# Attention on one core: maxima 4 units ahead instead of 6, rows turned two steps ahead instead of three, sums over V in halves in plain steps

## The chip, the cores and the metric

The kernel runs on one core of a Trainium2 chip. The metric is the device time of one execution in microseconds (us), the median of three runs. A core has TensorE (PE in the rows, its weight loads PEld), VectorE (DVE), ScalarE (ACT), GpSimd (POOL) and SyncE (SP), each with its own queue of instructions, worked through in order and held together by semaphores, and 16 DMA engines that they share.

## What is computed

Two transformer layers on x of 2 x 1024 x 288, each modulated by a condition vector. Both begin with an attention of 16 heads of 18 columns; layer 0 goes on with a dense MLP, layer 1 with a mixture of 4 experts of which each token takes 2. The change is in the attention alone, which is the same in both layers:

```python
qkv = (h @ W_qkv + b_qkv).reshape(B, N, 3, 16, 18)       # B = 2, N = 1024
scores = einsum('bhqd,bhkd->bhqk', q, k) * 18 ** -0.5
attn = softmax(scores, axis=-1)
o = einsum('bhqk,bhkd->bhqd', attn, v).reshape(B, N, 288)
x = x + gate * (o @ W_proj + b_proj)
```

## The kernel before, in words

`attention_stage` is called once for each layer. Its work is cut into 16 **spans**: 8 groups of 4 heads (`GROUPS`), each for 2 halves of 512 queries (`HALVES`). A span has 8 **steps** (`KT`), one for each block of 128 keys, so a layer has 128 steps.

Queries and keys lie as fp32r parts, two heads to a tile, one head in rows 0 to 55 and one in rows 64 to 119 (`QS`, `KS`). A step computes, for the 4 heads of its group:

- the scores of 128 keys against 512 queries, one matmul a head (`score`, L1101), into one of 3 PSUM banks `psS`. The maximum of each query is subtracted by the matmul itself, through two more rows of `QS` that hold the negated maxima in two parts;
- the exponentials of each, by ScalarE, from PSUM into `PR` (L972);
- the sums over V (`weigh`, L1112) of the step before: four matmuls of 32 output columns, which fill the array side by side (`tile_position=(0, 32 * j)`), accumulated over the 8 steps of a span in the bank `psO`. V holds a column of ones, so the sums of exponentials come out as well.

The maxima need a pass of their own. A **unit** is 128 queries of one head against all 1024 keys: two matmuls of 512 keys (`max_half`, L1062) into one of the two double banks `psM`, and one reduction on VectorE (L987). A span needs 16 units, and each step does two of them for a later span. `AHEAD` says how many units beyond the first span's 16 are done before the first step. When the 16 units of a span are through, `turn` (L1072) transposes the 128 x 16 maxima into the ring `psM`, VectorE splits them into two parts (`rows_out`, L997 and L999), SyncE stores them with four DMAs into the rows of `QS` (`store_max`, L832), and the first `score` of the span waits for these DMAs (`m_loaded`). `TURN_LEAD` says at the end of which step `turn` stands, counted back from the span's first. `spread` (L1081) is the matmul that spreads the inverted sums of the span before, at the end of a span's step 7 (`SPREAD_LAG`), and `divide` (L1017) uses it. SyncE's other work in a span is the load of the sums (L841) and two stores of their inverses (L846), around steps 1 to 5.

The order on each engine is written out by hand. On TensorE a step reads score 0, first half of a unit, score 1, second half, score 2, first half of the next unit, score 3, second half, `weigh` of the step before, and then `turn` or `spread` where there is one. The heads are taken in the order 0, 2, 1, 3, and a unit is of the head in the other rows, so that a score and the half unit behind it use different rows of the array and run together. I call such a couple a pair; a step has pairs 0 to 3. The waits that matter here:

```python
pe.wait_ge(exp_done, HG * st + n - 2)     # score(st, n): bank free, i.e. exponential of three scores ago done
pe.wait_ge(ring_read, ring - 1)           # max_half(q, 0): reduction of two units ago done
pe.wait_ge(exp_done, HG * (st + 1))       # weigh(st): all four exponentials of its step
pe.wait_ge(m_loaded[half], 64 * g + 64)   # score(8 * span, 0): the span's maxima are in QS
```

`TAIL` is the first step that has no units left. Spans, steps and pairs are counted from 0.

Of the kernel before, what the change touches and what calls it, by code (L numbers as in the profile page):

```python
# [32 lines left out]
BLK = 512  # L33
# [5 lines left out]
HG = 4  # L39
GPB = H // HG  # L40
GROUPS = B * GPB
KT = SEQ // P
# [655 lines left out]
STEPS = SPANS * KT  # L698
UNITS = HG * TPB
PER_STEP = UNITS // KT  # L700
AHEAD = 6
TURN_LEAD, COPY_LAG, RECIP_LAG, SPREAD_LAG = 3, 1, 4, 7


def unit_at(q):
# [6 lines left out]
def units_of(st):  # L712

    first = UNITS + AHEAD + PER_STEP * st
    return range(first, min(first + PER_STEP, SPANS * UNITS))
# [10 lines left out]
def span_turned(st):  # L726

    span, rest = divmod(st + TURN_LEAD, KT)
    return span if rest == 0 and 0 < span < SPANS else None
# [33 lines left out]
def attention_stage(nc, T, l, W, pieces):  # L763
# [4 lines left out]
    with ExitStack() as ctx:  # L768
# [276 lines left out]
        def _(pe):  # L1045
# [56 lines left out]
                                 QS[g % SLOTS][rows, half, p, :], start=True, stop=True  # L1102
                                 ).then_inc(scores_ready, 1)

            def weigh(st):
                span, k = divmod(st, KT)
                g = span // HALVES
                if k == 0 and span:
                    pe.wait_ge(oz_ready, span)
                pe.wait_ge(exp_done, HG * (st + 1))  # L1110
                for j in range(HG):
                    last = nc.tensor.matmul(psO[32 * j:32 * j + 32, :], T.V[:, g, k, 32 * j:32 * j + 32],  # L1112
                                            PR[st % 2][:, j, :], start=(k == 0), stop=(k == KT - 1),
                                            tile_position=(0, 32 * j))
                last.then_inc(pv_done, 1)

            def unit(q):
                max_half(q, 0)
# [5 lines left out]
                    turn(0)  # L1124
            for st in range(STEPS):
                units = list(units_of(st))
                score(st, 0)
                if units:
                    max_half(units[0], 0)
                score(st, 1)  # L1130
                if units:
                    max_half(units[0], 1)
                score(st, 2)
                if units:
                    max_half(units[1], 0)
                score(st, 3)
                if units:
                    max_half(units[1], 1)
                if st:
                    weigh(st - 1)  # L1140
                if (span := span_turned(st)) is not None:
                    turn(span)
                if (span := span_behind(st, SPREAD_LAG)) is not None:
                    spread(span)
            weigh(STEPS - 1)
            pe.wait_ge(oz_ready, SPANS)
            ring_free()
            nc.tensor.matmul(psM[ring % 2][:, 0, :], T.sel[:], OZ[HALVES - 1][:], start=True, stop=True
# [998 lines left out]
```

## Time and profile before

| what | us |
|---|---|
| median of three runs (lowest, highest) | 1590.88 (1589.6, 1596.12) |
| the profiled execution's own time | 1594.51 |
| its span, first to last instruction | 1592.8 |
| attention of layer 0, first reduction to last exponential | 136.0 to 514.7 |
| attention of layer 1, the same | 791.1 to 1172.6 |

The profile is of one execution. Its page gives the busy time of each engine; the timeline gives each instruction's start and length, and in brackets how long its engine had been idle and what ended that. TensorE's clock is granted at 1.00 (2.4 GHz) or 0.50 (1.2 GHz). A TensorE record's end is modelled, so its start is the better mark, and a matmul whose weights were not loaded ahead starts together with its weight load. An fp32 matmul stands in the records as two, which is why `weigh` has x8 in the timeline and x2048 on the page.

### The profile page before, as it was taken

To read this page: it belongs to the slowest core of one execution; us is meant where nothing else is said; L and a number is where in the kernel's file an instruction comes from. 1 tells how busy PE (TensorE), PEld (TensorE's weight loads), DVE (VectorE), ACT (ScalarE), POOL (GpSimd) and SP (SyncE) were. 2 spreads that over 40 slices of the span, in tenths; PEclk is the share of its full clock that TensorE was granted. 3 is DMA by queue.
4 is the path that set the end of the run, shared out by engine and by line. 5 is a ranking of instruction groups with operands and counts; after the bars stand their busy time and mean duration, and the time that the engine had idled before them with its cause. 6 is when DMAs were issued, how large, how long until landed. Compare 5 with 4: busy or idle time off the path is not lost. (4 is left out here: it accounts for less than half of the span.)

```text
span 1592.8 us, 25033 instructions
## 1 busy us (share of the span) xinstructions
PE 1383.1 (87%) x8657; PEld 867.5 (54%) x8657; DVE 1132.8 (71%) x1859; ACT 798.8 (50%) x1537; POOL 643.0 (40%) x857
## 2 busy tenths in 40 slices
PE   4686899999999879968799999999987299999995
PEld 2463333333332668856533333333335299999995
DVE  3756799999993546776489999999827456666663
ACT  0440577777778242224337677777854233332331
POOL 0433654431000515542469889888005511212121
PEclk7796899999999979989869999999998599999997
DMA  7475544331100249516561122220039456767672
GB/s 191 135 197 123 121 86 131 96 77 26 24 3 3 79 140 320 170 48 206 168 109 30 32 36 47 48 48 3 3 125 337 161 177 214 216 208 223 201 219 77
DMA packets 92740, 193.31 MB, mean 121 GB/s; under 512 B 35670, under 2 KB 62360, under 8 KB 89628
## 3 DMA queue, kind: packets, MB, share of 16 engines
q1 hardware_dynamic: 61020, 118.75, 23.2%
q0 software_dynamic: 31600, 73.00, 19.9%
q8 instruction: 70, 1.15, 0.3%
q14 instruction: 50, 0.41, 0.1%
HBM read 126.10 MB, written 66.67 MB: 121 GB/s over the span
## 5 line engine op out<-in xcount | busy, mean ns | idle before, releaser
L987 DVE TENSOR_REDUCE att_neg_max<-att_for_max 128x1 f32<-128x1024 f32 x512 | 601.0, 1219 | 74.2 <-PE att_for_max L1062 71.6
L972 ACT ACTIVATE att_probs<-att_scores 128x512 f32<-128x512 f32 x1002 | 525.1, 607 | 216.1 <-PE att_scores L1101 215.3
L1112 PE MATMUL att_out<-att_probs,V 128*32 128x512 f32 x2048 | 276.2, 612 | 2.9 <-ACT att_OZ L965 1.9
L1062 PE MATMUL att_for_max<-att_KS,att_QS 54*128 54x512 f32 x640 | 241.6, 461 | 3.7 <-DVE att_neg_max L987 2.5
L1101 PE MATMUL att_scores<-att_QS,att_KS 56*128 56x512 f32 x618 | 227.7, 450 | 18.2 <-ACT att_probs L972 16.1
L1101 PEld LDWEIGHTS att_scores<-att_QS,att_KS 56*128 56x128 f32 x618 | 101.8, 184 | 174.7 <-ACT att_probs L972 158.3
L1948 ACT ACTIVATE experts_gelu<-experts_proj,experts_b 128x256 f32<-128x256 f32 x171 | 81.3, 476 | 207.6 <-PE experts_proj L2017 186.8
L1062 PE MATMUL att_for_max<-KS,QS 54*128 54x512 f32 x384 | 162.8, 526 | 21.1 <-PEq L119 11.1
L2017 PE MATMUL experts_proj<-experts_x_parts,w_parts 128*128 128x256 f32 (+1 forms) x1197 | 173.9, 286 | 1.4 <-DVE experts_x_parts L1742 1.4
L1896 POOL DMA_INDIRECT sums_of_experts<-experts_y,experts_rows x38 | 61.1, 1607 | 259.2 <-DVE experts_y L1778 253.4
L2017 PEld LDWEIGHTS experts_proj<-experts_x_parts,w_parts 128*128 128x128 f32 (+1 forms) x1197 | 157.8, 191 | 5.4 <-issue 5.4
L1101 PE MATMUL att_scores<-QS,KS 56*128 56x512 f32 x384 | 147.1, 456 | 13.9 <-ACT att_probs L972 10.8
L1750 DVE CAST perts_hidden_parts<-experts_gelu 128x256 fp32r<-128x256 f32 x171 | 51.7, 302 | 110.9 <-ACT experts_gelu L1948 91.4
L1101 PEld LDWEIGHTS att_scores<-QS,KS 56*128 56x128 f32 x384 | 67.3, 190 | 109.6 <-ACT att_probs L972 93.2
L1062 PEld LDWEIGHTS att_for_max<-att_KS,att_QS 54*128 54x128 f32 x640 | 105.7, 185 | 24.1 <-DVE att_neg_max L987 19.1
L897 POOL TENSOR_TENSOR att_router_products<-att_router_products 128x576 f32<-128x576 f32 (+1 forms) x224 | 110.8, 495 | 17.6
L456 POOL DMA_DIRECT2D att_QS<-qk_halves x120 | 74.3, 653 | 107.2 <-PE att_scores L1101 81.3
L1062 PEld LDWEIGHTS att_for_max<-KS,QS 54*128 54x128 f32 x384 | 70.9, 217 | 57.9 <-DVE att_neg_max L987 43.9
L681 PE MATMUL qkv_qk<-qkv_hT_parts,qkv_wqkv_parts 128*126 128x512 f32 (+2 forms) x280 | 70.4, 406 | 14.3 <-DVE qkv_hT_parts L415 9.2
L1112 PEld LDWEIGHTS att_out<-att_probs,V 128*32 128x32 f32 x2048 | 40.4, 108 | 71.3 <-ACT att_probs L972 48.8
L1752 DVE TENSOR_TENSOR perts_hidden_parts<-experts_gelu,perts_hidden_parts 128x256 fp32r<-128x256 f32 x171 | 72.8, 426 | 5.8
L456 POOL DMA_DIRECT2D QS<-qk_halves x72 | 44.4, 645 | 75.8 <-PE att_scores L1101 42.0
(244 smaller groups left out, 2048.6 us busy)
## 6 DMA issues: line engine op xcount, KB each, us to landing
w_parts<-w_parts SPq DMA_DIRECT2D x19, 2304.0 KB
qk_halves<-qkv_qk_parts SPq DMA_DIRECT2D x40, 288.0 KB
w_parts<-w_parts SPq DMA_DIRECT2D x4, 2592.0 KB
slot_rows<-mlp_blank_rows SPq DMA_DIRECT2D x2, 5145.0 KB, 38.6
att_QS<-qk_halves POOLq DMA_DIRECT2D x120, 72.0 KB, 4.5
att_KS<-qk_halves POOLq DMA_DIRECT2D x60, 144.0 KB, 4.9
w_parts<-w_parts SPq DMA_DIRECT2D x19, 432.0 KB
experts_rows<-slot_rows SPq DMA_DIRECT2D x19, 294.0 KB
```

The lines of the kernel that those rows point to most:

```text
L456: eng.dma_start(Q[rows, half, :, :].bitcast(F32), heads[0, q, i, :, :, half * BLK:(half + 1) * BLK]).then_inc(sem, 16)
L681: last = nc.tensor.matmul(psQ[c % QK_BANKS][0:r, :], w[0:rows, ws, c0:c0 + r], hT[0:rows, hs, at:at + BLK], start=(n == 0), stop=(n == len ...
L897: at = router(nc.gpsimd.tensor_tensor(prod[:, 0:half, :], prod[:, 0:half, :], prod[:, half:2 * half, :], ALU.add))
L972: nc.scalar.activation(PR[st % 2][:, j, :], score_bank(st, n), ACT.Exp, scale=SCALE).then_inc(exp_done, 1)
L987: nc.vector.tensor_reduce(negm[half][:, c:c + 1], psM[ring % 2][:].rearrange("p a n -> p (a n)"), AX_X, ALU.max, negate=True).then_inc(rin ...
L1062: last = nc.tensor.matmul(psM[ring % 2][:, keys, :], QS[s][rows, half, p, t * P:(t + 1) * P], KS[s][rows, p, keys * BLK:(keys + 1) * BLK], ...
L1101: nc.tensor.matmul(score_bank(st, n), KS[g % SLOTS][rows, p, k * P:(k + 1) * P], QS[g % SLOTS][rows, half, p, :], start=True, stop=True).t ...
L1112: last = nc.tensor.matmul(psO[32 * j:32 * j + 32, :], T.V[:, g, k, 32 * j:32 * j + 32], PR[st % 2][:, j, :], start=(k == 0), stop=(k == KT ...
L1752: nc.vector.tensor_tensor(hp[k % RING][:, 1, :], g32[k % RING][:], hp[k % RING][:, 0, :].bitcast(F32), ALU.subtract).then_inc(parts_ready, 1)
L1896: nc.gpsimd.indirect_dma_start(T.acc[:, :], bass.IndirectOffsetOnAxis(xg[b % XG][:, t, ID_AT:ID_AT + 1].bitcast(U32), 0), y[b % 2][:, t, : ...
L1948: nc.scalar.activation(g32[k % RING][:], psH[k % RING][:, 0:EBLK], ACT.Gelu_apprx_tanh, bias=b1[:, ds(e * NF + f, 1)]).then_inc(gelu_ready, 1)
L2017: last = nc.tensor.matmul(psH[k % RING][:, 0:EBLK], w1[b % 2][0:rows, ws, f * P:(f + 1) * P], xT[b % 2][0:rows, hs, :], start=(n == 0), st ...
```

## The change

- `AHEAD` goes from 6 to 4: two units fewer before the first step, and each later unit one step later. `TAIL` moves from step 117 to step 118.
- `TURN_LEAD` goes from 3 to 2: `turn` stands at the end of step 6 of the span before, not step 5. The last maxima of a span now come in step 5, not step 4.
- `weigh` takes a range of query columns. In a **cut** step it runs twice, columns 0 to 255 between pairs 1 and 2, and columns 256 to 511 at the step's end. A step is cut where it has units, no `turn` and no `spread`, and is not one whose `weigh` is a span's first (step 1 of a span). That makes steps 0, 2, 3, 4 and 5 of a span, 75 steps in a layer. The semaphore waits stand ahead of the first half.

```diff
-AHEAD = 6
-TURN_LEAD, COPY_LAG, RECIP_LAG, SPREAD_LAG = 3, 1, 4, 7
+AHEAD = 4
+TURN_LEAD, COPY_LAG, RECIP_LAG, SPREAD_LAG = 2, 1, 4, 7
...
-            def weigh(st):
+            def weigh(st, n0, n1):
                 span, k = divmod(st, KT)
                 g = span // HALVES
-                if k == 0 and span:
-                    pe.wait_ge(oz_ready, span)
-                pe.wait_ge(exp_done, HG * (st + 1))
+                if n0 == 0:
+                    if k == 0 and span:
+                        pe.wait_ge(oz_ready, span)
+                    pe.wait_ge(exp_done, HG * (st + 1))
                 for j in range(HG):
-                    last = nc.tensor.matmul(psO[32 * j:32 * j + 32, :], T.V[:, g, k, 32 * j:32 * j + 32],
-                                            PR[st % 2][:, j, :], start=(k == 0), stop=(k == KT - 1),
-                                            tile_position=(0, 32 * j))
-                last.then_inc(pv_done, 1)
+                    last = nc.tensor.matmul(psO[32 * j:32 * j + 32, n0:n1], T.V[:, g, k, 32 * j:32 * j + 32],
+                                            PR[st % 2][:, j, n0:n1], start=(k == 0 and n0 == 0),
+                                            stop=(k == KT - 1 and n1 == BLK), tile_position=(0, 32 * j))
+                if n1 == BLK:
+                    last.then_inc(pv_done, 1)
...
             for st in range(STEPS):
                 units = list(units_of(st))
+                plain = span_turned(st) is None and span_behind(st, SPREAD_LAG) is None
+                cut = BLK // 2 if units and plain and st and (st - 1) % KT else 0
...
                     max_half(units[0], 1)
+                if cut:
+                    weigh(st - 1, 0, cut)
                 score(st, 2)
...
                 if st:
-                    weigh(st - 1)
+                    weigh(st - 1, cut, BLK)
```

On TensorE, a plain step in the middle of a layer (L1101 are the scores, L1062 the half units, L1112 the sums over V), before:

```order
L1101 MATMUL att_scores<-att_QS,att_KS 128x512
L1062 MATMUL att_for_max<-KS_0,QS_0 128x512
L1101 MATMUL att_scores<-att_QS,att_KS 128x512
L1062 MATMUL att_for_max<-KS_0,QS_0 128x512
L1101 MATMUL att_scores<-att_QS,att_KS 128x512
L1062 MATMUL att_for_max<-KS_0,QS_0 128x512
L1101 MATMUL att_scores<-att_QS,att_KS 128x512
L1062 MATMUL att_for_max<-KS_0,QS_0 128x512
L1112 MATMUL att_out<-att_probs,V 32x512 x4
```

and now, where the line of the sums is L1113:

```order
L1101 MATMUL att_scores<-att_QS,att_KS 128x512
L1062 MATMUL att_for_max<-KS_0,QS_0 128x512
L1101 MATMUL att_scores<-att_QS,att_KS 128x512
L1062 MATMUL att_for_max<-KS_0,QS_0 128x512
L1113 MATMUL att_out<-att_probs,V 32x256 x4
L1101 MATMUL att_scores<-att_QS,att_KS 128x512
L1062 MATMUL att_for_max<-KS_0,QS_0 128x512
L1101 MATMUL att_scores<-att_QS,att_KS 128x512
L1062 MATMUL att_for_max<-KS_0,QS_0 128x512
L1113 MATMUL att_out<-att_probs,V 32x256 x4
```

Half of the sums moved between the second and the third pair of a step.

On VectorE, two spans of layer 0 (L987 are the reductions, two a step; L1006 to L1010 invert the sums of the span before, in step 4; L997 and L999 split the turned maxima, and SyncE's four DMAs wait for L999; L1017 divides, in step 7), before:

```order
L987 TENSOR_REDUCE att_neg_max<-att_for_max 128x1 x14
L1006 RECIPROCAL att_inverse<-att_sums 128x16
L1008 CAST att_inverse_parts<-att_inverse 128x16
L1010 TENSOR_TENSOR att_inverse_parts<-att_inverse,att_inverse_parts 128x16
L987 TENSOR_REDUCE att_neg_max<-att_for_max 128x1 x2
L997 CAST att_neg_max_rows<-att_for_max 16x128
L999 TENSOR_TENSOR att_neg_max_rows<-att_for_max,att_neg_max_rows 16x128
L987 TENSOR_REDUCE att_neg_max<-att_for_max 128x1 x4
L1017 TENSOR_TENSOR heads_out<-att_OZ,att_for_max 128x512
```

and now:

```order
L987 TENSOR_REDUCE att_neg_max<-att_for_max 128x1 x12
L1006 RECIPROCAL att_inverse<-att_sums 128x16
L1008 CAST att_inverse_parts<-att_inverse 128x16
L1010 TENSOR_TENSOR att_inverse_parts<-att_inverse,att_inverse_parts 128x16
L987 TENSOR_REDUCE att_neg_max<-att_for_max 128x1 x4
L997 CAST att_neg_max_rows<-att_for_max 16x128
L999 TENSOR_TENSOR att_neg_max_rows<-att_for_max,att_neg_max_rows 16x128
L987 TENSOR_REDUCE att_neg_max<-att_for_max 128x1 x2
L1017 TENSOR_TENSOR heads_out<-att_OZ,att_for_max 128x512
```

Two reductions, one step, moved from behind the split of the maxima to ahead of it: between L999 and L1017 stand the reductions of one step, where there were two.

## Rows read from the trace of the kernel before

**Rows 1.** The page, busy time and share of the span of each engine

```profile
PE 1383.1 (87%) x8657; PEld 867.5 (54%) x8657; DVE 1132.8 (71%) x1859; ACT 798.8 (50%) x1537; POOL 643.0 (40%) x857
```

**Rows 2.** Page, costliest groups: xcount | busy us, mean ns | idle before <- releaser

```profile
L987 DVE TENSOR_REDUCE att_neg_max<-att_for_max 128x1 f32<-128x1024 f32 x512 | 601.0, 1219 | 74.2 <-PE att_for_max L1062 71.6
...
L1112 PE MATMUL att_out<-att_probs,V 128*32 128x512 f32 x2048 | 276.2, 612 | 2.9 <-ACT att_OZ L965 1.9
```

**Rows 3.** Timeline of one plain step: start, length, engine, line, operation, [idle before <- releaser]

```profile
308.83 0.18 PEld L1101 LDWEIGHTS att_scores<-QS,KS 56*128 56x128 f32 x1 [0.84 <-ACT att_probs L972]
...
309.17 0.39 PE L1101 MATMUL att_scores<-QS,KS 56*128 56x512 f32 x1
...
309.40 0.40 PE L1101 MATMUL att_scores<-QS,KS 56*128 56x512 f32 x1
...
309.42 2.07 ACT L972 ACTIVATE att_probs<-att_scores 128x512 f32<-128x512 f32 x4 [0.60 <-PE att_scores L1101]
...
309.63 2.36 DVE L987 TENSOR_REDUCE att_neg_max<-att_for_max 128x1 f32<-128x1024 f32 x2 [0.31 <-PE att_for_max L1062]
310.07 0.18 PEld L1101 LDWEIGHTS att_scores<-QS,KS 56*128 56x128 f32 x1 [0.52 <-ACT att_probs L972]
...
310.49 0.16 PEld L1112 LDWEIGHTS att_out<-att_probs,V 128*32 128x32 f32 x8 [0.24 <-issue]
...
311.49 0.18 PEld L1101 LDWEIGHTS att_scores<-QS,KS 56*128 56x128 f32 x1 [0.84 <-ACT att_probs L972]
```

**Rows 4.** Timeline from the turned rows of a span to its first scores

```profile
228.38 0.28 PE L1072 MATMUL att_for_max<-ident,att_neg_max 128*16 128x128 f32 x1
228.58 0.18 PEld L1101 LDWEIGHTS att_scores<-att_QS,att_KS 56*128 56x128 f32 x1
...
228.96 0.27 DVE L997 CAST att_neg_max_rows<-att_for_max 16x128 fp32r<-16x128 f32 x1
...
229.57 2.75 SPq L832 DMA_DIRECT2D att_QS<-att_neg_max_rows  x4
...
231.26 0.18 PEld L1101 LDWEIGHTS att_scores<-att_QS,att_KS 56*128 56x128 f32 x1 [0.84 <-ACT att_probs L972]
...
233.94 0.49 PE L1081 MATMUL att_for_max<-att_inverse_rows,sel_parts 128*128 128x512 f32 x1
...
234.36 0.18 PEld L1101 LDWEIGHTS att_scores<-att_QS,att_KS 56*128 56x128 f32 x1 [0.24 <-issue]
```

**Rows 5.** Timeline of the maxima ahead of the first step, two units apart

```profile
138.50 1.23 DVE L987 TENSOR_REDUCE att_neg_max<-att_for_max 128x1 f32<-128x1024 f32 x1 [0.18 <-PE att_for_max L1062]
...
141.03 1.23 DVE L987 TENSOR_REDUCE att_neg_max<-att_for_max 128x1 f32<-128x1024 f32 x1 [0.17 <-PE att_for_max L1062]
```

**Rows 6.** Timeline of the last span's turned rows, in the steps without maxima

```profile
492.73 0.28 PE L1072 MATMUL att_for_max<-ident,att_neg_max 128*16 128x128 f32 x1
...
493.05 0.28 DVE L997 CAST att_neg_max_rows<-att_for_max 16x128 fp32r<-16x128 f32 x1 [1.21 <-PE att_for_max L1072]
...
497.59 0.73 PE L1101 MATMUL att_scores<-att_QS,att_KS 56*128 56x512 f32 x3 [0.46 <-DMA att_QS<-att_neg_max_rows]
```

**Rows 7.** Timeline of TensorE around its two longest idle times in attention

```profile
189.09 0.50 PE L1101 MATMUL att_scores<-QS,KS 56*128 56x512 f32 x1 [2.45 <-DMA QS<-att_neg_max_rows]
...
192.63 0.79 PE L1101 MATMUL att_scores<-QS,KS 56*128 56x512 f32 x1
...
881.80 0.28 PE L1072 MATMUL att_for_max<-ident,att_neg_max 128*16 128x128 f32 x1 [1.60 <-DVE att_neg_max L987]
```

**Rows 8.** By stretch: length, busy PE, PEld, DVE, ACT, POOL, clock, DMA share, GB/s

```profile
187.30:190.70 3.40, 1.33 (x8) 0.67 (x8) 0.80 (x1) 1.01 (x3) 3.01 (x3) 1.00 0.23 97
190.70:194.10 3.40, 3.40 (x16) 1.03 (x14) 1.73 (x3) 1.63 (x5) 1.06 (x2) 0.50 0.69 220
...
880.20:883.60 3.40, 1.38 (x8) 0.89 (x9) 3.11 (x6) 0.72 (x2) 3.09 (x5) 1.00 0.25 37
883.60:887.00 3.40, 3.40 (x17) 0.99 (x17) 2.36 (x2) 1.56 (x3) 2.86 (x8) 0.50 0.02 5
```

More of the change, by code:

```diff
@@ L1144, in _ @@
                     spread(span)
-            weigh(STEPS - 1)
+            weigh(STEPS - 1, 0, BLK)
             pe.wait_ge(oz_ready, SPANS)
```

## The prediction, on record before the changed kernel ran

> **What bounds the kernel now.** The page comes first: TensorE is busy for 87% of the span and VectorE for 71% [rows 1], and the two costliest groups that the change touches are the 512 reductions of the maxima, with 74.2 us of idle VectorE before them, and the sums over V [rows 2]. That is an average, so I read one plain step next, in the timeline [rows 3]. It lasts 2.66 us, from the weight load of its first score at 308.83 to that of the next step at 311.49, and no engine is full in it. VectorE does two reductions in 2.36 us and then idles 0.31. ScalarE does four exponentials in 2.07 and idles 0.60. TensorE's weight loads wait 0.52 us ahead of pair 3, at 310.07, for an exponential.
>
> The chain that closes the step goes around: first score loaded at 308.83, first exponential at 309.42 (0.59 later), its bank free for pair 3 at 310.07 (1.24 after the step's start), the sums' weights at 310.49 (0.42 later), the next step at 311.49 (1.00 later). 1.24 + 0.42 + 1.00 = 2.66. Pair 3 waits for an exponential, and the whole block of sums stands behind it.
>
> The third view is the stretch from a span's turned maxima to its first score [rows 4]. `turn` runs at 228.38, VectorE's split begins at 228.96, SyncE issues four DMAs from 229.57 on, and the span's first score loads at 234.36, released by nothing that a DMA did: 5.98 us after `turn`, two steps. Where the steps are shorter, at the end of a layer, the same stretch took 4.86 us (492.73 to 497.59), and there the score did wait for the DMA [rows 6].
>
> **The halves in plain steps.** They put half of the sums into the 0.5 us in which TensorE waits for the exponential. What they cost is one more change between pairs and sums. I work out TensorE's own time. Pairs follow one another by 0.23 us (309.17 to 309.40), and a lone pair, from its weight load to that of the sums, took 0.42 [rows 3]. So two pairs and the change to the sums take 0.42 + 0.23 = 0.65. The full sums took 1.00, of which the first weight loads are 0.16 [rows 3]; only the rest halves, so half sums take 0.16 + 0.84 / 2 = 0.58. A cut step is then 2 x (0.65 + 0.58) = 2.46 us, all of it TensorE's. The other waits stay covered: the fourth exponential of the step before starts about 2.3 us into it by my count (pair 3 at 1.34, its scores out within 1.0) and ends about 0.45 us into the next, before the first half wants it at 0.65; pair 3 comes at about 1.34, after the 1.24 at which its bank is free; and VectorE needs 2.36 of the 2.46. A cut step so gains 2.66 - 2.46 = 0.20 us. The bounds: nothing, if the second change eats the idle time whole (it may take 0.35 of the 0.5 by my count), and 0.30, where VectorE's 2.36 us for two reductions becomes the limit. I take 0.20, since every piece of it has a row. There are 75 cut steps in a layer; 74 have a full step to compare with. 148 x 0.20 = **-29.6 us**.
>
> A rule of the Trainium skill speaks here. The rows show that the sums' weights were not loaded until pair 3's stream was over, 0.42 us after that pair's own load, though their wait had long ended [rows 3]. The page "TensorE: Matmul & The Clock Gate", in Part 3, The mechanism, says that TensorE pulls a weight load ahead of running matmuls when the row groups don't conflict or when it goes to the background weight buffer. The sums use all rows, so by its first case the trace agrees with it; by its second the loads would be hidden, which is a rival below.
>
> **Two units less ahead.** Before the first step VectorE takes 2.53 us for two units (138.50 to 141.03), and nothing runs beside it [rows 5]. Those two units move into a step with its own scores. 2 x 2.53 = **-5.1 us**.
>
> **The turn one step later.** This edit costs. What lies between `turn` and the span's first score was two steps and is now one. The step after `turn` took 231.26 - 228.58 = 2.68, and `spread` is still in the other [rows 4]. So without any wait the first score would now come 5.98 - 2.68 = 3.30 us after `turn`. But the data need longer: the layer's end shows 4.86 us from `turn` to the score that its DMA released, and there VectorE, which had nothing else, began its split 0.32 us after `turn`; in an ordinary span it begins 0.58 after, behind a reduction [rows 4, 6]. 4.86 + 0.26 = 5.12. SyncE is free at that point, as its stores of the inverses are one step further away than before. The wait is 5.12 - 3.30 = 1.82 us, and behind the waiting score stand the half units and the sums of the last step, so VectorE and ScalarE run dry as well. Spans 1 to 14 of both layers are 28 places; in span 1 of layer 0 the score waited for a late DMA already (2.45 us) [rows 7], so I count 27. 27 x 1.82 = **+49.1 us**. Bounds of one: 1.56, if the split begins as early as at the layer's end, and 2.2, if the split is later or a DMA waits behind GpSimd's.
>
> At the end of a layer the last span's wait existed before, at 4.86 us after `turn`. It stays, but `turn` comes after one more step, and that is a cut one: 2 x 2.46 = **+4.9 us**.
>
> Transfers that were late and had 0.9 us of cover (5.98 - 5.12) now show in full. I have no row for how many there are but the one in 30 spans that was late enough to show [rows 7]. I put **+2 us**, bounds 0 and +8.
>
> **The clock.** [rows 7] [rows 8] In attention TensorE was idle twice for over 1.5 us, 2.45 and 1.60, and both times the granted clock fell to 0.50 for the next 3.4 us after a stretch in which TensorE had been busy for 1.33 and 1.38 of 3.40. The price is in the rows: from the first score at 189.09 to the next step's at 192.63 are 3.54 us instead of 2.66, and that next matmul took 0.79 instead of 0.50. That is 0.88 + 0.29, about 1.2 us a fall. The new waits of 1.82 us lie between those two idle times, so some of the 28 will bring a fall. [...] I take 9 of 28: 9 x 1.2 = **+10.8 us**, bounds 0 and 28 x 1.2 = 34.
>
> **Sum.** -29.6 - 5.1 + 49.1 + 4.9 + 2 + 10.8 = +32.1 us. Against the profiled execution's 1594.5 that is 1626.6. The median of the runs lies 3.6 below that execution, so I predict **1623 us**. A measurement can tell this kernel from no change at about 0.5%, 8 us.
>
> **Rivals.**
> 1. The same waits, but no falls of the clock. [...] Time: 1623 - 10.8 = 1612, and 1610 without the late transfers.
> 2. The clock falls after most of the waits, 20 to 28 of them: 1612 + 24 to 34, which is 1636 to 1646. For it: two idle times over 1.5 us, two falls.
> 3. The halves bring nothing, because the second change takes all the idle time: 1623 + 29.6 = 1653, or 1642 without falls. For it: my estimate leaves only 0.2 of 0.55. Against it: each piece of it is a measured one.
> 4. Faster: the weights of the sums and of the pair behind them are loaded ahead at the new changes. Then TensorE needs about 2 x (0.23 + 0.23 + 0.42) = 1.76 us in a cut step and is no longer the limit. VectorE is, and two reductions that are always ready would start 1.14 us apart (2.36 less the 1.22 of one) [rows 2, 3], 2.28 a step. The gain is 0.38 x 148 = 56 us, against +48.9 of the waits, the layers' ends and the units ahead: -7.4, so 1584 us. It decides from a cut step of 2.66 - 48.9 / 148 = 2.33 us on down. Against it: no weight load was ahead at such a change before [rows 3]. This is what the second case of the Trainium skill's rule above would make of it.
> 5. About no change: cut steps at VectorE's 2.36 us (-44), waits near 1.56 (27 x 1.56 = 42), no falls: 1591 - 44 - 5 + 42 + 5 = 1589 to 1596, with the late transfers.
> 6. The edit doesn't act: the semaphore that the score waits for is set by the last DMA, and no cover but one step is left, so I see no way for the wait to be absent, and give it nothing.
>
> **Chances.** The forecast 35%, rival 1 27%, rival 2 18%, rival 3 8%, rival 5 7%, rival 4 5%. The forecast and rivals 1 to 3 are all slower by over 0.5%, that is above 1598.8 us: 0.88. Rival 5 is the same: 0.07. Rival 4 is faster: 0.05. The range leaves out rivals 3 and 4, most of 5, and the top of 2: 1600 to 1643 us. Its ends are the forecast with waits at 1.56, a cut gain of 0.25 and no falls (1610 - 7 - 7, rounded up for the late transfers), and with 25 falls.
>
> **What would show it.** Of the changed profile: a plain step of 2.46 us between two first scores, with the weight loads of half sums 0.65 us after the step's start. At every span's start the first score with an idle TensorE of about 1.8 us before it, released by the DMA of the maxima, 5.1 us after `turn`. Two layer starts 2.5 us shorter. Spans that last 22.0 - 5 x 0.20 + 1.8 = 22.8 us. The granted clock at 0.50 after some of the waits, and 1.2 us more in those spans. I am wrong in the sign if cut steps are below 2.33 us, or if the score at a span's start finds its DMA landed less than 4 us after `turn`; and wrong in the size if the clock falls nearly always or never.

## The result, and the profile after

The changed kernel takes 1679.3 us (median of four runs, 1670.1 to 1686.4) against 1590.2 us before: a ratio of 1.055, with a 95% interval of 1.049 to 1.061. That is slower by 89 us. I had forecast slower, at 1623 us and 1643 at most. The sign and the main wait were right; the size was not, and it lies above even the rival with a fall of the clock at nearly every span (1646).

The profiled execution took 1686.4 us, 91.9 more than the one before. The layers' attentions grew from 378.8 to 429.9 us and from 381.5 to 424.0 (first reduction to last exponential), together 93.6; everything else is as it was. From the page after, the line of busy times and the costliest groups (in the columns of [rows 2]):

```profile
PE 1441.8 (86%) x9857; PEld 869.4 (52%) x9857; DVE 1138.9 (68%) x1859; ACT 814.5 (48%) x1537; POOL 643.0 (38%) x857
...
L987 DVE TENSOR_REDUCE att_neg_max<-att_for_max 128x1 f32<-128x1024 f32 x512 | 612.1, 1222 | 150.9 <-PE att_for_max L1062 149.5
L972 ACT ACTIVATE att_probs<-att_scores 128x512 f32<-128x512 f32 x1004 | 540.6, 601 | 294.0 <-PE att_scores L1101 283.5
L1113 PE MATMUL att_out<-att_probs,V 128*32 128x256 f32 (+1 forms) x3248 | 337.0, 490 | 2.5 <-ACT att_OZ L965 1.6
L1101 PE MATMUL att_scores<-att_QS,att_KS 56*128 56x512 f32 x620 | 247.7, 489 | 43.9 <-DMA att_QS<-att_neg_max_rows 43.5
```

The work is hardly more, the idle time is: ahead of the reductions VectorE idled 74.2 us before [rows 2] and 150.9 now. Ahead of the scores TensorE waited for the maxima's DMAs. Who waited for these DMAs, before (us, times):

```profile
  PE att_scores L1101: 3.4, 3
```

and after:

```profile
  PE att_scores L1101: 68.1, 32
```

That is TensorE's own idle time. It stood in three places and was 3.4 us before; it is in all 32 spans now, 68.1 us.

**A plain step** in the timeline of layer 0 answers to [rows 3]:

```profile
455.00 0.18 PEld L1101 LDWEIGHTS att_scores<-att_QS,att_KS 56*128 56x128 f32 x1 [0.84 <-ACT att_probs L972]
...
455.60 2.26 ACT L972 ACTIVATE att_probs<-att_scores 128x512 f32<-128x512 f32 x4 [0.17 <-PE att_scores L1101]
455.66 0.16 PEld L1113 LDWEIGHTS att_out<-att_probs,V 128*32 128x32 f32 x8 [0.36 <-ACT att_probs L972]
...
455.80 2.46 DVE L987 TENSOR_REDUCE att_neg_max<-att_for_max 128x1 f32<-128x1024 f32 x2 [0.37 <-PE att_for_max L1062]
456.23 0.18 PEld L1101 LDWEIGHTS att_scores<-att_QS,att_KS 56*128 56x128 f32 x1 [0.41 <-ACT att_probs L972]
...
456.89 0.16 PEld L1113 LDWEIGHTS att_out<-att_probs,V 128*32 128x32 f32 x8 [0.37 <-issue]
...
457.46 0.18 PEld L1101 LDWEIGHTS att_scores<-att_QS,att_KS 56*128 56x128 f32 x1 [0.41 <-ACT att_probs L972]
```

It lasts 2.46 us (455.00 to 457.46), as predicted to the hundredth. The sums' weights come 0.66 us after the pairs, and the next pair 0.57 and 0.57 after them (I had 0.65 and 0.58). VectorE's two reductions start 1.24 us apart here and the next one 1.23 later, each as its operand comes. Reductions that find it ready start 1.14 apart, in this trace and in the one before (the 2.36 of [rows 3]), so it is TensorE that sets the 2.46 us of a cut step, and VectorE is close behind. The weight loads still wait for the stream before them at both changes. Of the rule of the Trainium skill (page "TensorE: Matmul & The Clock Gate", Part 3, The mechanism), the trace agrees with the case of conflicting row groups and shows none of a load into the background buffer here. That the row groups are what the loads wait for was not tried.

**From the turned rows to a span's first score**, which answers to [rows 4]:

```profile
444.80 0.28 PE L1072 MATMUL att_for_max<-ident,att_neg_max 128*16 128x128 f32 x1
...
445.27 0.27 DVE L997 CAST att_neg_max_rows<-att_for_max 16x128 fp32r<-16x128 f32 x1
...
445.88 2.75 SPq L832 DMA_DIRECT2D att_QS<-att_neg_max_rows  x4
...
447.69 0.50 PE L1081 MATMUL att_for_max<-att_inverse_rows,sel_parts 128*128 128x512 f32 x1
...
449.81 0.50 PE L1101 MATMUL att_scores<-att_QS,att_KS 56*128 56x512 f32 x1 [1.63 <-DMA att_QS<-att_neg_max_rows]
```

`turn` at 444.80, the split 0.47 later, SyncE's four DMAs from 445.88 on, `spread` at 447.69, and the score at 449.81 after 1.63 us of idle TensorE, released by the DMA: 5.01 us after `turn`. I had 5.12.

**The clock.** Stretches of 3.4 us around one such wait, with their columns:

```profile
core 0: us, PE busy (x) PEld busy (x) DVE busy (x) ACT busy (x) POOL busy (x), PEclk, DMA share, GB/s
289.20:292.60 3.40, 1.76 (x13) 0.46 (x13) 2.62 (x3) 1.14 (x3) 3.03 (x2) 1.00 0.04 10
292.60:296.00 3.40, 3.40 (x20) 1.21 (x24) 1.37 (x2) 1.69 (x4) 2.06 (x3) 0.50 0.28 55
296.00:299.40 3.40, 3.40 (x20) 1.31 (x16) 2.46 (x3) 2.27 (x5) 0.00 (x0) 0.50 0.57 207
299.40:302.80 3.40, 3.40 (x20) 0.70 (x12) 1.63 (x2) 1.83 (x4) 0.00 (x0) 0.50 0.02 2
302.80:306.20 3.40, 3.40 (x36) 1.33 (x36) 3.01 (x3) 2.45 (x6) 0.00 (x0) 0.99 0.00 0
```

and TensorE in them:

```profile
292.48 0.71 PE L1101 MATMUL att_scores<-att_QS,att_KS 56*128 56x512 f32 x1 [1.64 <-DMA att_QS<-att_neg_max_rows]
...
296.73 0.79 PE L1101 MATMUL att_scores<-att_QS,att_KS 56*128 56x512 f32 x1
...
300.85 0.79 PE L1101 MATMUL att_scores<-att_QS,att_KS 56*128 56x512 f32 x1
```

After the wait (1.64 us, with 1.76 of 3.40 busy) the clock is at 0.50 for three stretches in a row. A cut step takes 4.25 us in it (292.48 to 296.73, its first 0.12 still at full clock) instead of 2.46, and a whole one 4.12 (296.73 to 300.85) instead of 2.73. In the kernel before a fall lasted one stretch [rows 8]. The trace's record of the granted clock has 21 falls between each layer's second span and its end, of 3.4, 6.8 or 10.2 us, where there were 2.

Twenty of the 21 began during TensorE's idle time ahead of a span's first score or at most 1.9 us after it. The other one followed 0.77 us of waiting for a reduction (fall at 1142.5). These idle times are of two kinds. Thirteen are of 1.77 us and more, nearly all where a transfer was late or the layer ends, and all 13 were followed by a fall. Sixteen are of 1.60 to 1.66 us, and 7 of these were. In the one place of the 30 with a short wait, 0.28 us, there was none. The two attentions without their first span, after:

```profile
188.20:563.10 374.90, 339.90 (x2469) 122.88 (x2467) 285.02 (x308) 262.13 (x495) 83.77 (x119) 0.89 0.22 51
891.60:1262.90 371.30, 336.60 (x2469) 121.97 (x2469) 291.46 (x308) 263.40 (x495) 231.98 (x388) 0.91 0.14 27
```

A mean clock of 0.89 over 374.9 us and 0.91 over 371.3 is some 146 us at half clock by the trace's record; before it was 7 us.

### The profile page after: what moved, and what is told of

Its sections match the earlier page's. It is cut to its first block and busy times, and to the rows that moved or that the text cites. A ratio compares the mean times of both kernels' runs of the same rounds, so it can differ in the third digit from the quotient of the medians.

```text
span 1684.7 us, 27433 instructions
## 1 busy us (share of the span) xinstructions
PE 1441.8 (86%) x9857; PEld 869.4 (52%) x9857; DVE 1138.9 (68%) x1859; ACT 814.5 (48%) x1537; POOL 643.0 (38%) x857
## 5 line engine op out<-in xcount | busy, mean ns | idle before, releaser
L987 DVE TENSOR_REDUCE att_neg_max<-att_for_max 128x1 f32<-128x1024 f32 x512 | 612.1, 1222 | 150.9 <-PE att_for_max L1062 149.5
L972 ACT ACTIVATE att_probs<-att_scores 128x512 f32<-128x512 f32 x1004 | 540.6, 601 | 294.0 <-PE att_scores L1101 283.5
L1113 PE MATMUL att_out<-att_probs,V 128*32 128x256 f32 (+1 forms) x3248 | 337.0, 490 | 2.5 <-ACT att_OZ L965 1.6
L1101 PE MATMUL att_scores<-att_QS,att_KS 56*128 56x512 f32 x620 | 247.7, 489 | 43.9 <-DMA att_QS<-att_neg_max_rows 43.5
L1062 PE MATMUL att_for_max<-att_KS,att_QS 54*128 54x512 f32 x640 | 252.4, 483 | 5.2 <-DVE att_neg_max L987 4.4
L1101 PEld LDWEIGHTS att_scores<-att_QS,att_KS 56*128 56x128 f32 x620 | 103.5, 201 | 186.5 <-ACT att_probs L972 130.7
L1062 PE MATMUL att_for_max<-KS,QS 54*128 54x512 f32 x384 | 168.8, 546 | 19.3 <-PEq L119 10.6
L1101 PE MATMUL att_scores<-QS,KS 56*128 56x512 f32 x384 | 160.4, 496 | 25.3 <-DMA QS<-att_neg_max_rows 24.6
L1113 PEld LDWEIGHTS att_out<-att_probs,V 128*32 128x32 f32 x3248 | 66.5, 112 | 159.9 <-issue 86.4
L456 POOL DMA_DIRECT2D att_QS<-qk_halves x120 | 74.3, 652 | 141.6 <-PE att_scores L1101 69.8
L1101 PEld LDWEIGHTS att_scores<-QS,KS 56*128 56x128 f32 x384 | 67.9, 206 | 111.3 <-ACT att_probs L972 75.2
L1062 PEld LDWEIGHTS att_for_max<-att_KS,att_QS 54*128 54x128 f32 x640 | 105.6, 200 | 21.6 <-DVE att_neg_max L987 18.1
L1062 PEld LDWEIGHTS att_for_max<-KS,QS 54*128 54x128 f32 x384 | 71.9, 230 | 50.6 <-DVE att_neg_max L987 37.4
L681 PE MATMUL qkv_qk<-qkv_hT_parts,qkv_wqkv_parts 128*126 128x512 f32 (+2 forms) x280 | 72.3, 416 | 12.4 <-DVE qkv_hT_parts L415 10.2
L456 POOL DMA_DIRECT2D QS<-qk_halves x72 | 44.3, 644 | 87.8 <-PE att_scores L1101 54.2
```

The source lines that it names most:

```text
L456: eng.dma_start(Q[rows, half, :, :].bitcast(F32), heads[0, q, i, :, :, half * BLK:(half + 1) * BLK]).then_inc(sem, 16)
L681: last = nc.tensor.matmul(psQ[c % QK_BANKS][0:r, :], w[0:rows, ws, c0:c0 + r], hT[0:rows, hs, at:at + BLK], start=(n == 0), stop=(n == len ...
L972: nc.scalar.activation(PR[st % 2][:, j, :], score_bank(st, n), ACT.Exp, scale=SCALE).then_inc(exp_done, 1)
L987: nc.vector.tensor_reduce(negm[half][:, c:c + 1], psM[ring % 2][:].rearrange("p a n -> p (a n)"), AX_X, ALU.max, negate=True).then_inc(rin ...
L1062: last = nc.tensor.matmul(psM[ring % 2][:, keys, :], QS[s][rows, half, p, t * P:(t + 1) * P], KS[s][rows, p, keys * BLK:(keys + 1) * BLK], ...
L1101: nc.tensor.matmul(score_bank(st, n), KS[g % SLOTS][rows, p, k * P:(k + 1) * P], QS[g % SLOTS][rows, half, p, :], start=True, stop=True).t ...
```

## Experiments

Every ratio is against the kernel before, run beside it. That kernel's own median lay between 1590.2 and 1594.3 us from one session to another, so a difference of medians from two sessions can be off by up to 4 us from this alone. "Falls" are counted from a layer's second span on, both layers together.

### The halves alone

```diff
-AHEAD = 4
-TURN_LEAD, COPY_LAG, RECIP_LAG, SPREAD_LAG = 2, 1, 4, 7
+AHEAD = 6
+TURN_LEAD, COPY_LAG, RECIP_LAG, SPREAD_LAG = 3, 1, 4, 7
```

> The halves in plain steps alone, with the maxima 6 units ahead and the rows turned three steps ahead as before. Theory (the halves save 0.20 us a cut step and the lead of two steps is what costs): the five cut steps of a span are 2.46 us, no wait over 0.1 us at a span's start except the last, hardly a fall of the clock, so 148 x 0.20 = 30 us less than before: about 1561 us. Rival (the halves themselves bring the clock down, since TensorE changes between pairs and sums twice as often): the granted clock is at 0.50 in many places without any long wait, and the time is 1590 us or more.

Measured: 1590.1 us, ratio 1.000 (0.998 to 1.002). Neither came true. The waits are gone and the clock stays up (2 falls, as before), so the rival's condition isn't met though its time is, and nothing is gained. Steps 2 to 4 of a span are 2.46 us as expected. In layer 0 step 6, which stands behind `turn`, went from 2.67 to 3.28, and a span from 22.05 to 21.93 us. In layer 1 the step with `turn` got longer as well, 2.88 to 3.28, and a span went from 22.36 to 22.46: there the halves lose. In step 6 a half unit waits for a reduction:

```profile
357.54 0.50 PE L1062 MATMUL att_for_max<-att_KS,att_QS 54*128 54x512 f32 x1 [0.33 <-DVE att_neg_max L987]
```

### The change without the halves

```diff
-                cut = BLK // 2 if units and plain and st and (st - 1) % KT else 0
+                cut = 0
```

> The changed kernel with all sums over V whole (no cut steps), 4 units ahead and two steps of lead. Without falls of the clock the sum is 1612 + 30 = 1642 us. Theory (a fall of the clock is dear because a cut step has no idle TensorE left to pay it with): falls are as many as in the changed kernel, but each costs the 1.2 us that I read before, so 1650 to 1670 us, below the changed kernel's 1679. Rival (a fall costs the same with and without halves): 1679 + 30 = about 1709 us.

Measured: 1684.8 us, ratio 1.058 (1.054 to 1.062), 24 falls. It lies between the two theories. Beside 1679.3, the halves are worth 5.5 us in the changed kernel, which is not clear of the noise of the two ratios.

```profile
189.50:563.00 373.50, 330.74 (x1909) 122.41 (x1909) 281.58 (x308) 254.75 (x495) 84.36 (x120) 0.91 0.22 51
889.80:1269.30 379.50, 333.49 (x1909) 124.61 (x1907) 286.82 (x308) 255.34 (x495) 232.53 (x389) 0.91 0.14 26
```

By the trace's record it spent 133 us at half clock, in falls that are shorter than the changed kernel's. Steps that lie wholly at half clock show what the halves do there. A first step of a span takes 4.32 us cut (the changed kernel) and 4.13 whole (this one):

```profile
319.95 0.79 PE L1101 MATMUL att_scores<-QS,KS 56*128 56x512 f32 x1 [2.07 <-DMA QS<-att_neg_max_rows]
...
324.27 0.79 PE L1101 MATMUL att_scores<-QS,KS 56*128 56x512 f32 x1
```

```profile
1074.21 0.79 PE L1101 MATMUL att_scores<-att_QS,att_KS 56*128 56x512 f32 x1 [2.38 <-DMA att_QS<-att_neg_max_rows]
...
1078.34 0.79 PE L1101 MATMUL att_scores<-att_QS,att_KS 56*128 56x512 f32 x1
```

At full clock a cut step gains 0.20 us on a whole one; at half clock it loses 0.19.

### TensorE kept busy while it waits

```diff
+FILLS = 3
...
                 if k == 0 and n == 0:
+                    if span:
+                        pe.wait_ge(exp_done, HG * st - 2)
+                        for fill in range(FILLS):
+                            nc.tensor.matmul(score_bank(st, 0)[:, 0:BLK // 2], T.V[:, g, 0, :], T.V[:, g, 0:2, :],
+                                             start=True, stop=True)
                     pe.wait_ge(m_loaded[half], 64 * g + 64)
```

> The changed kernel, but TensorE runs three more fp32 matmuls of 128 x 256 on V ahead of each span's first score, into the bank that this score overwrites, so that it is busy while it waits for the maxima. They should take about 1.4 us of the 1.7 us wait and no time of their own. Theory (what my sum misses, 1679 - 1612 = 67 us, is the clock that falls after the idle waits): the granted clock stays at 1.00 through the middle of both attentions and the time is 1610 to 1625 us, with the waits still there. Rival (the missing time is in longer transfers or in the cut steps): 1670 us or more.

Measured: 1630.7 us, ratio 1.023 (1.019 to 1.028), 4 falls. In its timeline the extra matmuls stand where the idle time was, and the score waits for the DMA as before:

```profile
421.45 1.46 PE L1094 MATMUL att_scores<-V 128*128 128x256 f32 x6
423.23 0.49 PE L1107 MATMUL att_scores<-att_QS,att_KS 56*128 56x512 f32 x1 [0.32 <-DMA att_QS<-att_neg_max_rows]
```

The clock in its two attentions:

```profile
189.10:535.60 346.50, 333.94 (x2553) 132.21 (x2553) 284.99 (x308) 261.85 (x495) 84.33 (x120) 0.98 0.24 55
862.10:1215.60 353.50, 335.88 (x2553) 132.64 (x2553) 287.58 (x308) 262.51 (x495) 232.30 (x390) 0.98 0.16 28
```

This is the run that settles where most of the missing time was. The change did more work on TensorE and ended 48.6 us earlier, with the waits as long as ever. The expected 1610 to 1625 was missed by 6 us. Late transfers (below) are still there, and all 4 falls follow one: TensorE idled 1.69, 1.86, 2.82 and 3.15 us ahead of them, in spite of the extra matmuls.

### The same, without the halves

The two edits above together.

> The changed kernel without cut steps and with TensorE kept busy by three extra matmuls ahead of each span's first score. Against the filled kernel with halves (1631 us) it shows what the halves are worth when the clock hardly falls; unfilled, the two kernels were equal (1679 and 1685). Theory (a span is waiting for its maxima for 1.7 us in any case, in which VectorE catches up, so here the cut steps' 0.20 us come through): 28 x 0.75 = 21 us slower than 1631, about 1652 us. Then the halves lose this gain unfilled because the clock stays low for longer after a fall. Rival (the halves are worth nothing in any surroundings): 1631 to 1637 us.

Measured: 1654.1 us, ratio 1.037 (1.034 to 1.039), 6 falls, as the theory had it. The four kernels make a table:

| us | TensorE idle in the wait | filled |
|---|---|---|
| sums in halves | 1679.3 | 1630.7 |
| sums whole | 1684.8 | 1654.1 |

The halves are worth 23.4 us where the clock stays up and 5.5 where it falls. The falls cost 48.6 us with halves and 30.7 without. Divided by the falls that the filling took away, 17 and 18, that is 2.9 us a fall with halves and 1.7 without. The four kernels did not all run in one session. Taken as distances from the kernel before in its own session, the four differences are 19.8, 5.0, 49.1 and 34.3 us, and the prices 2.9 and 1.9 us. The order is the same.

### One extra matmul instead of three

> The changed kernel with one extra matmul instead of three ahead of each span's first score: TensorE idles about 1.2 us instead of 1.7 there, and the wait for the maxima is as long as ever. Theory (it is the length of the idle time that makes the clock fall): most of the 21 falls go, and the time is 1635 to 1650 us. Rival (any idle time over 1 us does it): falls as often as in the changed kernel, 1670 us or more.

Measured: 1654.2 us, ratio 1.038 (1.036 to 1.041), 11 falls. It is a little above the theory's range and far from the rival. The maxima come as late after `turn` in all three kernels; what differs is how long TensorE idles before them. In 19 of the 30 places it now idled 1.14 to 1.23 us, and no fall followed one of these. Ten of the 11 falls followed the places where a transfer was late or the layer ends, with 1.78 us idle and more. Counted in all three kernels, places with a fall of all places:

| TensorE idle ahead of a span's first score, us | changed kernel | one extra | three extra |
|---|---|---|---|
| 1.69 to 4.79 | 13 of 13 | 10 of 11 | 4 of 4 |
| 1.57 to 1.66 | 7 of 16 | none such | 0 of 1 |
| 1.14 to 1.41 | none such | 0 of 19 | 0 of 4 |
| under 1 | 0 of 1 | none such | 0 of 21 |

One more fall in each of the first two came in a step with `turn`, behind a wait for a reduction. So the length decides, as the theory has it, and the wait of 1.6 us that the changed kernel has in an ordinary span lies where it can go either way. It isn't this idle time alone, though: with the sums whole and three extra matmuls, 5 of 9 places with 1.11 to 1.40 us idle were followed by a fall. There TensorE is busy for only 2.46 us of a plain step's 2.66, and a cut step has it busy throughout.

### GpSimd's loads behind the maxima

```diff
                     pool.wait_ge(scores_ready, (g - SLOTS + 1) * HALVES * KT * HG)
+                    pool.wait_ge(m_loaded[0], 64 * (g - SLOTS + 2))
```

In the changed kernel some transfers were late. The timeline ahead of span 6 of layer 1:

```profile
1014.91 2.75 SPq L832 DMA_DIRECT2D QS<-att_neg_max_rows  x4
...
1016.41 1.21 POOL L456 DMA_DIRECT2D att_QS<-qk_halves  x2 [9.72 <-PE att_scores L1101]
...
1020.15 0.79 PE L1101 MATMUL att_scores<-QS,KS 56*128 56x512 f32 x1 [2.92 <-DMA QS<-att_neg_max_rows]
```

GpSimd's loads of a later group (L456, L458) begin at 1016.41, when the scores of the span are done. SyncE's four DMAs of the maxima are under way then, and the score gets its maxima after 2.92 us of idle TensorE, not 1.6. The kernel before issued the maxima a step earlier, and GpSimd's loads began at about the time they landed. In most even spans that was 4.9 to 5.5 us after `turn`; the loads now begin 2.2 to 2.6 us after it.

> The changed kernel, but GpSimd's loads of a later group wait for the maxima of the next span as well as for the scores of the last one. In the changed kernel these loads (18 DMAs a group) start while the maxima's four DMAs are under way, in the even spans, and there the last of the four lands 5.4 to 7.5 us after the rows are turned instead of 4.96. Theory (GpSimd's DMAs hold the maxima up): the even spans' step 7 goes from 5 to 8 us down to 4.8, which is 10 to 15 us in all, and the falls of the clock that followed the longer waits get fewer or shorter; 1655 to 1668 us. Rival (the late landings have another cause): about 1679 us, and steps of over 5 us remain.

Measured: 1659.7 us, ratio 1.045 (1.040 to 1.050), 15 falls: the theory. The same place in it, where GpSimd now waits:

```profile
991.07 2.75 SPq L832 DMA_DIRECT2D QS<-att_neg_max_rows  x4
...
994.99 0.50 PE L1102 MATMUL att_scores<-QS,KS 56*128 56x512 f32 x1 [1.63 <-DMA QS<-att_neg_max_rows]
...
995.58 0.61 POOL L456 DMA_DIRECT2D att_QS<-qk_halves  x1 [7.04 <-PE att_scores L1102]
```

The steps 7 ahead of the even spans 2 to 14 sum up to 68.9 us instead of 79.5. The other 9 us I put down to the falls, 15 instead of 21. Three long steps 7 remain in layer 0 (7.19, 6.12 and 5.28 us). GpSimd's DMAs of split weights run there, and that they are the cause wasn't tried.

### Six units ahead, two steps of lead

> The changed kernel with 6 units ahead instead of 4. My sum had -5.1 us for the two units. Theory (the first score of a layer waits for the first span's maxima in both, 28.0 us after the first reduction, so units ahead of it are free): within 3 us of the changed kernel's 1679 us, up or down. Rival (the units are worth their 2.5 us a layer): 1684 us or more.

Measured: 1674.4 us, ratio 1.053 (1.050 to 1.057); the changed kernel had 1.055 (1.049 to 1.061). It is 2 us outside the 3 that the theory allowed, on the side that speaks against the rival even more, and not clear of noise. The trace settles it: from a layer's first reduction to its first exponential it is 28.06 and 28.04 us here, 28.04 and 27.94 in the changed kernel. The two units are worth nothing there.

### Four units ahead, three steps of lead

```diff
-TURN_LEAD, COPY_LAG, RECIP_LAG, SPREAD_LAG = 2, 1, 4, 7
+TURN_LEAD, COPY_LAG, RECIP_LAG, SPREAD_LAG = 3, 1, 4, 7
```

> The changed kernel with the rows turned three steps ahead, as before, and 4 units ahead. The rows are then turned at the end of the very step that has their last reduction, so TensorE has to wait for it, about 0.8 us a span, but not for the maxima at the span's start. Theory (it is the lead that costs): no wait over 1 us at a span's start, hardly a fall of the clock, 1590 + 28 x 0.8 = 1612 us at most and 1595 at least. Rival (4 units ahead cost on their own, at the span's start): over 1640 us.

Measured: 1614.1 us, ratio 1.014 (1.012 to 1.016), 5 falls. The step with `turn` took 3.98 us instead of 2.87, since TensorE waited 1.1 us there for the last reduction, not 0.8. So 4 units are too few for three steps of lead, which is why the change took both numbers down together. What it paid for is the lead.

### Two stores instead of four

```diff
-                for i in range(2):
-                    for e in range(2):
-                        at = i * LANES + ROWS + e
-                        sp.dma_start(QS[g % SLOTS][at:at + 1, half, :, :].bitcast(F32),
-                                     mrow[i * UNITS // 2:(i + 1) * UNITS // 2, e, :].bitcast(F32)
-                                     ).then_inc(m_loaded[half], 16)
+                for e in range(2):
+                    sp.dma_start(QS[g % SLOTS][slice(ROWS + e, P, LANES), half, :, :].bitcast(F32),
+                                 mrow[:, e, :].bitcast(F32)).then_inc(m_loaded[half], 16)
```

with 32 for 64 in the waits for `m_loaded`.

> The changed kernel with the maxima stored by two DMAs instead of four (both row groups of the array in one), which should have the data in place 1.4 us earlier: 3.6 us after the rows are turned instead of 4.95. Theory (the wait at the span's start is what starts the falls): the wait shrinks from 1.7 to about 0.3 us, no fall follows it, and the time is 1612 - 27 x 1.4 = 1574 us, faster than before. Rival (the time of the two rows' DMAs is set by what is moved and not by their number): the wait stays near 1.7 us and the time near 1679 us.

Measured: 1585.2 us, ratio 0.996 (0.994 to 0.998). With two DMAs fewer to issue the step ahead of a span is 3.22 us instead of 4.79, and 2 falls are left, as in the kernel before. This one edit takes 94 us off the changed kernel. GpSimd's loads still begin 2.2 to 2.6 us after `turn` in even spans, but the maxima land 3.4 us after it there as in the others. It isn't 1574, because the span's first step then takes 2.82 us and its step with `turn` 3.27, with short waits for reductions in them: VectorE is behind.

### What bounds a span with halves

The halves alone, and the sums whole also in the step behind `turn`:

```diff
-                plain = span_turned(st) is None and span_behind(st, SPREAD_LAG) is None
+                plain = span_turned(st) is None and span_behind(st, SPREAD_LAG) is None and not (st and span_turned(st - 1) is not None)
```

> The halves alone (6 units ahead, three steps of lead), but the sums are also whole in the step behind `turn` (step 6 of a span), so that steps 0, 2, 3 and 4 are cut. With the halves alone a span took 21.93 us against 22.05, because step 6 took 3.28 us instead of 2.67 while steps 2 to 4 saved 0.20 each. Theory (VectorE is what a span with cut steps is bound by: it was idle for 1.05 us of 21.93, so what a step saves has to be waited for later): step 6 gets shorter but the others or the spread's step get longer, a span stays within 21.7 to 21.95 us, and the time is 1583 to 1590 us. Rival (the cut in step 6 itself is what costs 0.6 us, on TensorE): a span of 21.3 us, so 28 x 0.6 = 17 us less, about 1573 us.

Measured: 1582.2 us, ratio 0.993 (0.991 to 0.995). A span of layer 0 takes 21.70 us, at the lower edge of the theory's 21.7 to 21.95 (of layer 1, 22.2). Step 6 fell by 0.31 and not by 0.61, and the span's first step got longer by 0.05. One span of layer 0 before, in the columns of the stretches above:

```profile
345.05:367.09 22.04, 21.05 (x132) 8.50 (x131) 20.31 (x23) 17.02 (x33) 9.61 (x17) 1.00 0.46 83
```

with the halves alone:

```profile
341.17:363.10 21.93, 21.60 (x171) 8.13 (x170) 20.88 (x23) 17.65 (x33) 9.59 (x17) 1.00 0.47 84
```

and in this kernel:

```profile
342.66:364.38 21.72, 21.32 (x164) 8.19 (x163) 20.68 (x23) 17.55 (x33) 9.60 (x17) 1.00 0.38 85
```

VectorE was busy for 92% of the span before and is busy for 95% in both others. What the halves free on TensorE can only be used as far as VectorE keeps up. It isn't full in the cut steps, where its reductions start 1.23 us apart, as TensorE feeds them. It is nearly full behind them: from the inverses to `divide` its reductions start 1.13 us apart, and half units wait for them. So the 0.8 us that four cut steps should save shrinks to 0.35. That VectorE is what stops the rest is read from these waits; no run here made VectorE faster.

### The version that beats both

The last kernel with the two stores: 6 units ahead, three steps of lead, halves in steps 0, 2, 3 and 4.

> The kernel of the run before this one, with the maxima stored by two DMAs instead of four. The data are in place 1.4 us earlier. Theory (the DMAs of the maxima are on the path only ahead of a layer's first step and at its last span, and VectorE bounds the rest): 2 x 1.4 at the layers' starts and up to 2 x 0.5 at their ends less than the run before, 3 to 4 us. Rival (in ordinary spans too the score waits a little for the DMAs): 10 us less or more.

Measured: 1576.6 us, ratio 0.990 (0.988 to 0.993), 1 fall. That is 5.6 us less than the run before it, between the two expectations: next to the last spans of the layers, a late transfer in layer 0's first span is covered as well (its first score had waited 1.46 us). The 2 x 1.4 us at the layers' starts did not come: the first exponential is 28.03 us after the first reduction, as with four stores. In the changed kernel with two stores, which has 4 units ahead, it is 26.5. With the maxima in place sooner, the two units more are what the start waits for. Its attentions:

```profile
184.00:502.40 318.40, 311.96 (x2357) 117.70 (x2353) 284.42 (x307) 261.95 (x496) 86.71 (x121) 1.00 0.27 62
828.10:1154.90 326.80, 314.32 (x2357) 117.95 (x2353) 291.44 (x307) 262.06 (x496) 231.95 (x388) 0.99 0.18 30
```

## Why the prediction was wrong

By its own terms, each against what the runs showed:

| term | predicted | measured |
|---|---|---|
| halves in cut steps | -29.6 | -23.4 with the clock up |
| two units less ahead | -5.1 | 0 |
| wait at the spans' starts | +49.1 | 27 x (4.79 - 3.10) = +45.6 |
| late transfers | +2 | about +12 |
| layers' ends | +4.9 | about +6 |
| the clock | +10.8 | at least +48.6 |
| sum | +32.1 | +89 |

The measured column adds up to the 89 us between the medians. That close a match is partly luck, as three of its terms are differences of runs that are sure to a few us only. "Layers' ends" is read from the kernel with whole sums and filled waits, 2.84 us more from the start of span 14 to the last exponential of a layer than before.

- **The halves.** The cut step was right, 2.46 us. What failed is "The other waits stay covered": with 2.46 us a step VectorE has hardly any slack for the inverses, which it does in step 5. The reductions then run late into the step with `turn`, where a half unit's weights wait 0.61 us for one, and this step took 3.10 us instead of 2.88. That gives back about 28 x 0.22 = 6 us.
- **Two units less ahead.** This step was wrong as a step. I priced two reductions at 2.53 us a layer and read that "nothing runs beside" them. The first span's maxima did: its first score waited for their DMA, as it does now. In the changed kernel's timeline VectorE ends the last reduction ahead of the score at 159.54, and the score waits on:

```profile
157.18 2.36 DVE L987 TENSOR_REDUCE att_neg_max<-att_for_max 128x1 f32<-128x1024 f32 x2 [0.81 <-PE att_for_max L1062]
...
160.46 0.28 PEld L1101 LDWEIGHTS att_scores<-QS,KS 56*128 56x128 f32 x1 [3.54 <-DMA QS<-att_neg_max_rows]
```

  From a layer's first reduction to its first exponential it is 28.03 us before and 28.04 and 27.94 after.
- **The wait.** Right in place, cause and size: 5.01 us after `turn`, 1.69 us in the step's length.
- **Late transfers.** The step that failed was the count. I looked for transfers that had been late before. The moved ones collide with something new, GpSimd's loads at the end of every second span, and that follows from the diff: the turn moved past the point at which GpSimd is released. The steps 7 ahead of the spans 1 to 14 sum up to 146.9 us in both layers, where it was 88.9 before; 45.6 of these 58.0 us are the wait above. The late ones cost more than that: 10 of the 13 idle times of over 1.7 us are theirs, and each was followed by a fall.
- **The clock.** This term carries the error. I took 9 falls at 1.2 us. That 9 of the 28 waits would be followed by one rests on nothing that a run shows; 18 of them were, and with the layers' ends and a wait for a reduction there were 21. Filling the waits took 48.6 us off, 2.9 a fall. The price came from a kernel whose weight loads wait 0.5 us in each step, and from falls of 3.4 us. A cut step is TensorE's from end to end, so every pass that takes twice as long is paid: 2.46 becomes 4.32, where a whole step goes from 2.67 to 4.13. And the falls last longer. So the two parts of the change act against each other: the lead makes the clock fall, and the halves take away the slack that would have covered some of it. Why a fall lasts 3.4 us in one place and 10.2 in another I can't tell from these runs.
- **The rivals.** Rival 1 is out, with 21 falls. Rival 2 had the mechanism, but at my price of a fall its top was 1646. Rivals 3, 4 and 5 are out: the halves are worth 23 us filled, and no cut step was below 2.46.

## What to carry to other kernels

A wait that is added to TensorE near its limit costs its length, and may also cost the clock afterwards. Then every term of a sum that was read at full clock is wrong, most of all in the stretches where TensorE has no slack. A quick test is to give TensorE something useless to do in the wait. And before a transfer is moved, look at what the other queues issue at its new place, and at what the first consumer of a stage was really waiting for before work is taken out ahead of it.

## What the runs showed that I had not expected

- Where TensorE idled 1.60 to 1.66 us ahead of a span's first score, the granted clock fell in 7 places of 16. With 1.77 us and more it fell in 13 of 13, and with 1.14 to 1.23 us (one extra matmul) in none of 19.
- Time grew shorter with more work: three useless matmuls a span, 1.46 us of them, took 48.6 us off.
- A fall lasted up to 10.2 us although TensorE was busy without a break during it, 3.40 of 3.40 in each stretch.
- Sums in halves are faster at full clock (2.46 us a step for 2.67) and slower at half clock (4.32 for 4.13).
- The number of DMAs, not what they carry, set the time to the maxima: two that fill the same rows as four had them there 1.6 us sooner.
